# Relational graph layer on one core: nine masks instead of ten, and the mean taken off by ScalarE for a third of the dense tiles and for the finished rows

## The reference

```python
proj = einsum('ni,rio->nro', x, relation_weight)          # 10 matrices of 64 x 64
t_r, h_r = proj[src, etype], proj[dst, etype]
att = sum(t_r * tanh(h_r + edge_attr), -1)
a = softmax of att over the edges of one dst
h = segment_sum(x[src] * a, dst)                          # 0 for a node without edges
y = x + leaky((x + h) @ W.T) + leaky((x * h) @ W2.T)      # slope 0.01
out = (y - mean(y)) / sqrt(var(y) + 1e-5)                 # over the 64 values of a row
```

## Time and profile before

| | |
|---|---|
| median of 3 runs | 757.59 us (756.48 to 757.81) |
| the profiled execution | 757.37 us, its span 755.7 us |
| busy: PE, PEld, DVE, ACT, POOL | 567.3, 310.8, 628.0, 484.1, 569.9 us |
| mean granted TensorE clock | 0.930 |

### The profile page before, as it was taken

How to read it: one execution, slowest core, us unless ns; L and a number is a source line. 1 busy time by engine, 2 the same in 40 slices (tenths; PEclk the granted TensorE clock), 3 DMA queues, 4 the chain that set the end, 5 groups by cost and what they waited for, 6 DMA issues and landing times. The chain is left out here.

```text
span 755.7 us, 14910 instructions
## 1 busy us (share of the span) xinstructions
PE 567.3 (75%) x3948; PEld 310.8 (41%) x3948; DVE 628.0 (83%) x1118; ACT 484.1 (64%) x1432; POOL 569.9 (75%) x590
## 2 busy tenths in 40 slices
PE   1897888888888898888898796899988898853000
PEld 0652454454454454454454453444444443542000
DVE  2689899999999999999999999999998898862010
ACT  0376777778778788779779778655543555665040
POOL 6777777777777777777777777767777777777776
PEclk9999999999999999999999999999999999975555
DMA  4463434444434434434434424320222212100000
GB/s 120 112 188 83 122 99 138 113 110 137 124 100 138 124 96 139 124 97 141 134 85 147 113 56 123 98 77 28 76 76 74 75 37 80 45 27 18 18 18 16
DMA packets 49458, 70.44 MB, mean 93 GB/s; under 512 B 17450, under 2 KB 20966, under 8 KB 49374
## 3 DMA queue, kind: packets, MB, share of 16 engines
q1 hardware_dynamic: 30750, 52.33, 21.5%
q0 software_dynamic: 18624, 17.16, 11.0%
HBM read 45.61 MB, written 25.78 MB: 94 GB/s over the span
## 5 line engine op out<-in xcount | busy, mean ns | idle before, releaser
L454 POOL DMA_INDIRECT xsd<-in_x,ends_i x384 | 374.5, 975 | 118.0 <-issue 109.1
L556 PE MATMUL t_ps<-xm,w_rel 64*64 64x512 f32 (+1 forms) x1000 | 269.5, 621 | 42.0 <-DVE xm L963 41.2
L963 DVE SCALAR_TENSOR_TENSOR xm<-typ,xT_ps 128x1024 f32<-128x1024 f32 (+1 forms) x250 | 291.6, 1183 | 7.2 <-issue 7.2
L558 PE MATMUL h_ps<-xm,w_rel 64*64 64x512 f32 (+1 forms) x1000 | 269.5, 621 | 0.0
L478 POOL DMA_INDIRECT out<-out_r,row_i x196 | 192.3, 981 | 62.5 <-issue 56.7
L556 PEld LDWEIGHTS t_ps<-xm,w_rel 64*64 64x64 f32 x1000 | 52.8, 134 | 144.7 <-DVE xm L963 120.4
L573 PE MATMUL y_ps<-bd_cat,dT 128*128 128x256 f32 x392 | 97.0, 391 | 17.6 <-DVE zd L1025 14.9
L731 ACT ACTIVATE o_t<-zd,rstd 128x64 f32<-128x64 f32 x392 | 98.8, 337 | 15.4 <-DVE rstd L1047 15.3
L573 PEld LDWEIGHTS y_ps<-bd_cat,dT 128*128 128x128 f32 x392 | 71.8, 193 | 30.8 <-issue 12.9
L1005 DVE SCALAR_TENSOR_TENSOR es<-es,wd,wx 128x64 f32<-128x64 f32 x196 | 55.2, 281 | 11.2 <-DVE es L1005 0.5
L738 ACT ACTIVATE wd<-delta 128x16 f32<-128x16 f32 (+1 forms) x25 | 5.4, 216 | 88.2 <-DVE delta L993 83.8
(11 more groups left out here) (155 smaller groups left out, 844.8 us busy)
## 6 DMA issues: line engine op xcount, KB each, us to landing
xsd<-in_x SPq DMA_DIRECT2D x1024, 0.2 KB
x_in<-in_x SPq DMA_DIRECT2D x48, 256.0 KB
typ<-typ_d SPq DMA_DIRECT2D x24, 512.0 KB, 4.8
out<-o_t SPq DMA_DIRECT2D x48, 256.0 KB
xsd<-in_x,ends_i POOLq DMA_INDIRECT x384
hist<-es SPq DMA_DIRECT2D x24, 256.0 KB, 2.0
ea<-in_edge_attr SPq DMA_DIRECT2D x24, 224.0 KB
out<-out_r,row_i POOLq DMA_INDIRECT x196, 2.1
```

Of the source, the lines that this page charges most:

```text
L454: pool.indirect_dma_start(xsd[:, s % RX, j, side, :], None, x[:, :], bass.IndirectOffsetOnAxis(ap=ends_i[:, side, c:c + 1], axis=0),).then ...
L556: pe.matmul(t_ps[h * D:(h + 1) * D, 0:n], w_rel[0:D, r, :], xm[0:D, b, h * n:(h + 1) * n], start=(r == 0), stop=(r == R - 1), skip_group_c ...
L558: mm = pe.matmul(h_ps[(1 - h) * D:(2 - h) * D, 0:n], w_rel[D:P, r, :], xm[D:P, b, (1 - h) * n:(2 - h) * n], start=False, stop=(r == R - 1) ...
L963: v.scalar_tensor_tensor(xm[:, (s * R + r) % RM, 0:n], typ[:, s % RT, 0:n], float(r), xT_ps[:, 0:n], ALU.is_equal, ALU.mult).then_inc(mask ...
```

## The change

1. **Nine masks.** Since the ten types cover every edge, the sum over the ten masked products is x times `w_rel[9]` for all columns, plus the masked products of types 0 to 8 with `w_rel[r] - w_rel[9]`. The differences are made once at the start by DVE (`dif_done`, 128 x 576 elements). In each step ACT copies the whole of `xT_ps` (1024 columns) to a new tile `xc` (`plain(s)`, right after `tanh`), mask 0 waits for that copy instead of for `xT_done`, and PE's fifth quad of the step multiplies `xc`. PE's work keeps its size.
2. **Squares with a bias.** For the third tile of each step (`UNCENTRED`) and for the finished rows no mean is subtracted by DVE. ACT squares `zsum - 64 z`, 8 instructions of 64 columns with the row sum as bias, in place of one of 512; the other squares get the scale 64, and the root 1/64**3.
3. **The mean in the scaling.** A new small DVE instruction `shifts(s)` (128 x 32) gives -mean x rstd; `rec_done` now comes from it, one mask after the reciprocal. `dense_norm` of third tiles and `final_out` use `Identity` with scale and bias in place of `Copy` with scale.
4. `zf` becomes a ring of 3, and the sums stay in `zsum`, with waits for their readers.

```diff
+RF = 3
...
+    RB = R - 1
+    PLAIN_AT = 4
+
+    def quad_count(m):
+        return m // RB * R + m % RB + (2 if m % RB >= PLAIN_AT else 1)
+
+    UNCENTRED = [2]
+
+    def mids(d):
+        return sum(n % 3 not in UNCENTRED for n in range(d + 1))
...
+        xc = sb("xc", [P, COLS * P])
...
-                wait(pe, masked, s * R)
+                wait(pe, masked, s * RB)
...
-            def quad(s, r):
-                pe.wait_ge(masked, s * R + r + 1)
-                if r == 0:
+            def quad(s, at):
+                plain = at == PLAIN_AT
+                r = RB if plain else at - (at > PLAIN_AT)
+                if plain:
+                    pe.wait_ge(plain_done, s + 1)
+                else:
+                    pe.wait_ge(masked, s * RB + r + 1)
+                if at == 0:
                     wait(pe, prod_done, s)
-                b = (s * R + r) % RM
                 n = cols(s) // 2 * P
+                moving = xc[:, :] if plain else xm[:, (s * RB + r) % RM, :]
+                w = w_rel[:, r, :]
                 for h in range(2):
-                    pe.matmul(t_ps[h * D:(h + 1) * D, 0:n], w_rel[0:D, r, :], xm[0:D, b, h * n:(h + 1) * n],
-                              start=(r == 0), stop=(r == R - 1), skip_group_check=True)
-                    mm = pe.matmul(h_ps[(1 - h) * D:(2 - h) * D, 0:n], w_rel[D:P, r, :], xm[D:P, b, (1 - h) * n:(2 - h) * n],
-                                   start=False, stop=(r == R - 1), skip_group_check=True)
+                    pe.matmul(t_ps[h * D:(h + 1) * D, 0:n], w[0:D, :], moving[0:D, h * n:(h + 1) * n],
+                              start=(at == 0), stop=(at == R - 1), skip_group_check=True)
+                    mm = pe.matmul(h_ps[(1 - h) * D:(2 - h) * D, 0:n], w[D:P, :], moving[D:P, (1 - h) * n:(2 - h) * n],
+                                   start=False, stop=(at == R - 1), skip_group_check=True)
                 mm.then_inc(quad_done, 1)
...
+            pe.wait_ge(dif_done, 1)
...
+            def plain(s):
+                n = cols(s) * P
+                act.wait_ge(xT_done, s + 1)
+                wait(act, quad_done, (s - 1) * R + PLAIN_AT + 1 if s > 0 else 0)
+                act.copy(xc[:, 0:n], xT_ps[:, 0:n]).then_inc(plain_done, 1)
...
-                act.wait_ge(zmid_done, d + 1)
                 wait(act, dred_done, d - 1)
-                act.activation(sqd[:, d % 2, :], zd[:, d % RZ, :], ACT.Square).then_inc(dsq_done, 1)
+                if d % 3 in UNCENTRED:
+                    act.wait_ge(zsum_done, d + 1)
+                    for j in range(DR):
+                        ins = act.activation(sqd[:, d % 2, j * D:(j + 1) * D], zd[:, d % RZ, j * D:(j + 1) * D], ACT.Square,
+                                             scale=-float(D), bias=zsum[:, d // 3 % 2, d % 3, j:j + 1])
+                    ins.then_inc(dsq_done, 1)
+                else:
+                    act.wait_ge(zmid_done, mids(d))
+                    act.activation(sqd[:, d % 2, :], zd[:, d % RZ, :], ACT.Square, scale=float(D)).then_inc(dsq_done, 1)
 
             def dense_norm(d):
                 s = d // 3
                 act.wait_ge(rec_done, s + 1)
                 wait(act, o_stored[d % RO], d // RO * DMA)
-                for j in range(DR):
-                    ins = act.activation(o_t[:, d % RO, j * D:(j + 1) * D], zd[:, d % RZ, j * D:(j + 1) * D], ACT.Copy,
-                                         scale=rstd[:, s % 2, d % 3, j:j + 1])
+                if d % 3 in UNCENTRED:
+                    for j in range(DR):
+                        ins = act.activation(o_t[:, d % RO, j * D:(j + 1) * D], zd[:, d % RZ, j * D:(j + 1) * D], ACT.Identity,
+                                             scale=rstd[:, s % 2, d % 3, j:j + 1], bias=shift[:, s % 2, d % 3, j:j + 1])
+                else:
+                    for j in range(DR):
+                        ins = act.activation(o_t[:, d % RO, j * D:(j + 1) * D], zd[:, d % RZ, j * D:(j + 1) * D], ACT.Copy,
+                                             scale=rstd[:, s % 2, d % 3, j:j + 1])
                 ins.then_inc(dmul_done, 1)
...
-                act.activation(sd[:, s % 2, :, :], ssq[:, s % 2, :, :], ACT.Sqrt, scale=1.0 / D, bias=eps_t[:, 0:1]).then_inc(sqrt_done, 1)
+                act.activation(sd[:, s % 2, :, :], ssq[:, s % 2, :, :], ACT.Sqrt, scale=1.0 / D ** 3, bias=eps_t[:, 0:1]).then_inc(sqrt_done, 1)
...
             def final_square(f):
-                act.wait_ge(fsub_done, f + 1)
+                act.wait_ge(fsum_done, f + 1)
                 wait(act, red2_done, f)
-                act.activation(sqf[:, 0:cols(f), :], zcf[:, f % 2, 0:cols(f), :], ACT.Square).then_inc(fsq_done, 1)
+                for j in range(cols(f)):
+                    ins = act.activation(sqf[:, j, :], zf[:, f % RF, j, :], ACT.Square, scale=-float(D),
+                                         bias=zsum[:, f % 2, 3, j:j + 1])
+                ins.then_inc(fsq_done, 1)
 
             def final_out(f, s):
                 act.wait_ge(rec_done, s + 1)
                 if f >= RW:
                     act.wait_ge(scattered[f % RW], sum(cols(n) for n in range(f % RW, f, RW)) * DMA)
                 for j in range(cols(f)):
-                    ins = act.activation(out_r[:, f % RW, j, :], zcf[:, f % 2, j, :], ACT.Copy, scale=rstd[:, s % 2, 3, j:j + 1])
+                    ins = act.activation(out_r[:, f % RW, j, :], zf[:, f % RF, j, :], ACT.Identity,
+                                         scale=rstd[:, s % 2, 3, j:j + 1], bias=shift[:, s % 2, 3, j:j + 1])
                 ins.then_inc(fmul_done, 1)
...
+                if 0 <= s < NS:
+                    plain(s)
...
+            v.wait_ge(w_in, 5 * DMA)
+            v.tensor_tensor(w_rel[:, 0:RB, :], w_rel[:, 0:RB, :], w_rel[:, RB:R, :].to_broadcast([P, RB, D]), ALU.subtract).then_inc(dif_done, 1)
...
-                    v.wait_ge(xT_done, s + 1)
+                    v.wait_ge(plain_done, s + 1)
                     v.wait_ge(typ_in[s % RT], turn(s, RT) * DMA)
-                wait(v, quad_done, s * R + r + 1 - RM)
-                v.scalar_tensor_tensor(xm[:, (s * R + r) % RM, 0:n], typ[:, s % RT, 0:n], float(r), xT_ps[:, 0:n],
+                m = s * RB + r
+                wait(v, quad_done, quad_count(m - RM) if m >= RM else 0)
+                v.scalar_tensor_tensor(xm[:, m % RM, 0:n], typ[:, s % RT, 0:n], float(r), xT_ps[:, 0:n],
                                        ALU.is_equal, ALU.mult).then_inc(masked, 1)
...
             def dense_total(d):
                 v.wait_ge(zadd_done, d + 1)
-                v.tensor_reduce(zsd[:, :], zd[:, d % RZ, :].rearrange("p (j f) -> p j f", f=D), AX.X, ALU.add).then_inc(zsum_done, 1)
+                wait(v, rec_done, d // 3 - 1)
+                wait(v, dsq_done, d - 5)
+                v.tensor_reduce(zsum[:, d // 3 % 2, d % 3, :], zd[:, d % RZ, :].rearrange("p (j f) -> p j f", f=D), AX.X,
+                                ALU.add).then_inc(zsum_done, 1)
 
             def dense_centre(d):
                 v.wait_ge(zsum_done, d + 1)
                 z = zd[:, d % RZ, :].rearrange("p (j f) -> p j f", f=D)
-                v.scalar_tensor_tensor(z, zsd[:, :].unsqueeze(2).to_broadcast([P, DR, D]), -1.0 / D, z, ALU.mult, ALU.add).then_inc(zmid_done, 1)
+                v.scalar_tensor_tensor(z, zsum[:, d // 3 % 2, d % 3, :].unsqueeze(2).to_broadcast([P, DR, D]), -1.0 / D, z,
+                                       ALU.mult, ALU.add).then_inc(zmid_done, 1)
...
+                v.reciprocal(rstd[:, s % 2, :, :], sd[:, s % 2, :, :]).then_inc(rstd_done, 1)
+
+            def shifts(s):
+                v.wait_ge(rstd_done, s + 1)
+                v.scalar_tensor_tensor(shift[:, s % 2, :, :], zsum[:, s % 2, :, :], -1.0 / D, rstd[:, s % 2, :, :],
+                                       ALU.mult, ALU.mult).then_inc(rec_done, 1)
...
             def final_sum(f):
                 n = cols(f)
                 v.wait_ge(z2_done, f + 1)
-                v.tensor_reduce(zs[:, 0:n], zf[:, 0:n, :], AX.X, ALU.add).then_inc(fsum_done, 1)
-
-            def final_centre(f):
-                n = cols(f)
-                v.wait_ge(fsum_done, f + 1)
-                wait(v, fmul_done, f - 1)
-                v.scalar_tensor_tensor(zcf[:, f % 2, 0:n, :], zs[:, 0:n].unsqueeze(2).to_broadcast([P, n, D]), -1.0 / D,
-                                       zf[:, 0:n, :], ALU.mult, ALU.add).then_inc(fsub_done, 1)
...
                     restarts(e)
                 if ending:
                     pair(f)
-                if DP is not None:
-                    dense_centre(DP)
                 if main:
                     mask(s, 4)
-                if main:
-                    mask(s, 5)
                 if DP is not None:
                     dense_sum(DP)
                 if D0 is not None:
...
                     sum_one(e, 0)
                     sum_one(e, 1)
                 if main:
-                    mask(s, 6)
```

(46 more changed lines are left out.)

7 lines of the change are left out of this document (2 added, 5 removed).

## The result

The changed kernel takes 787.94 us, median of 4 runs (786.78 to 788.84), beside 757.7 for the kernel before on the same chip (756.48 to 758.19): a ratio of 1.0397, 95% interval 1.0385 to 1.0409. It is 30 us slower. The profiled execution took 787.24 us, its span is 785.5.

What follows compares the result with a forecast made beforehand. POOL's queue was taken to run to the end, with the steps acting only through the store it awaits. 22.8 + 1.6 + 2.4 = 26.8 us took the profiled 757.37 to 784.2, forecast 784, range 770 to 798.

Steps and rivals of the forecast that it cites:

- What bounds: POOL's gathers and scatters run to the end; steps count only through the store POOL awaits, set by tile 46's scaling.
- First stall: In each step DVE waits before `dense_sum(DP)` for ACT's eight-part square of the third tile: 1.04 us.
- second stall: In each step DVE waits before `dense_add(D1)` for ACT's relu, delayed by the finished rows' squares: 2.9 us.
- The small square: On ACT, each 64-column square with a bias costs 0.24 us start to start, about 2.0 us for eight.
- that rival: Small ACTIVATEs with a bias cost 0.30 us, not 0.24: 12 to 13 us more in all, 797; chance 0.12.
- DVE's own work in a step: DVE's queue without stalls falls from 28.28 to 26.1 us: 2.34 goes out, 0.20 for `shifts` comes in.
- Twelve steps: Steps 3 to 14 have all parts of the loss, each 1.9 us longer: 22.8 us in all.
- Step 15's part: Step 15 up to the end of tile 46's scaling grows from 22.2 to 23.8 us: 1.6 more.
- Start and steps 0 to 2: Weight differences at the start, up to 0.8 us, steps 1 and 2 each 1.0 longer, step 0 even: 2.4 together.
- POOL's hole: POOL's wait for the `o_t` store between gathers and scatters, 3.07 us before, grows to some 30 us.
- PACE's marks: PE's pace marks hold back POOL's gathers but add nothing, being reached well before the store lands.
- The other side's floor: If DVE's saving wins, POOL's hole closes and the time is 754.6 us, no better however short the step; chance 0.07.

Runs made afterwards that it cites:

- Experiment 3: The changed kernel with each set of eight small squares replaced by one instruction of 512 columns without a bias: 757.33 us, ratio 0.9995.
- experiment 7: The changed kernel with `Copy` and a scale alone in place of `Identity` with scale and bias: 781.49 us, ratio 1.0226.
- experiments 1: The kernel before with only the first part of the change (nine masks, plain copy, weight differences): 757.36 us, ratio 0.999.
- 4: The kernel before with nine masks and no mean taken off any dense tile (`dense_centre` gone): 760.61 us, ratio 1.0035.
- 12: The kernel before with only the first part of the change, and `final_out` moved ahead of `weights` in ACT's queue: 757.45 us, ratio 0.999.

## Why the prediction was right

The forecast of 784 stands beside 787.9 measured, and by its own steps:

- **What bounds.** Right: the end moved with the store of tile 48, through the end of tile 46's scaling (501.40, from 499.38 + 2.02 on ACT; predicted near 497) and SP's 24.3 us (24.4). From the first scatter to the end 256.5 in place of 257.8: 196 scatters took 191.0 us, 1.3 less than in the earlier trace rows.
- **First stall** 1.04 predicted, 0.95 measured; **second stall** 2.9 predicted, 3.28 measured. Both stand before the instructions named. Experiment 3 shows that the squares cause the first, and 1.7 us of the second (1.55 stay without them).
- **The small square** 0.24 from start to start: 2.00 to 2.01 for eight, with the bias from a tile. Right; for the squares that rival is out. It named `Identity` with both operands as well, and there it was half right: 2.74 for eight. The Trainium skill, page "ScalarE: Activation LUTs", section "Rules for kernel authors", would have 0.35 us each as an estimate. The trace has a mean duration of 0.33 to 0.34 for one, and 0.24 from start to start, since neighbours overlap: the estimate is near for the duration, and I was wrong to take it as the price of one in a row when I put the page's forecast 20 us later.
- **`shifts`** 0.20 predicted, 0.18. DVE's own work in a step 26.1 predicted, and 26.1 measured (30.34 less the two stalls). **`plain`** cost nothing, as said; it takes 1.01 us.
- **Twelve steps**: 22.8 predicted, 27.8 measured. This is the term that was too small. 2.9 of the 5.0 are four steps with parts at the lower granted clock (31.16, 30.94, 31.21 and 30.97 beside 30.34 for an undisturbed one). 0.8 is on the side of before, whose twelve steps averaged 28.21 and not the 28.28 that I had taken from the earlier trace rows, a stretch that begins in step 8, the one long step (28.56). The rest, 1.3, has two parts of opposite sign. `Identity` with two operands from tiles was costed like `Copy` with a scale; without it the step is 0.30 us shorter (30.04 beside 30.34, experiment 7), 3.0 us over ten steps. And that 30.04 is 0.16 under the 30.2 of my sum, some 1.9 over twelve steps. That they nearly cancel, and put 30.2 beside 30.34, was luck.
- **Step 15's part** 1.6 predicted, 1.5 (23.70 beside 22.19). **Start and steps 0 to 2** 2.4 predicted, 2.1.
- **POOL's hole.** Wrong: 9.11 us, not some 30. I had named PACE's marks as no term of the sum, and that holds. But the delay is spread: the gathers' busy time grew by 6.6 us and the idle time before them by 18.4, together 25.0, which is what the last gather came later (518.94 beside 493.89). The hole shows only what is left.
- **The other side's floor.** Wrong by 3 us: 754.6 supposed that POOL's last gather stays at 493.89 when steps get shorter. In experiments 1, 3, 4 and 12 it came at 497.4 to 500.3, mostly since single gathers took longer (983 to 988 ns on average, beside 975), and their medians are 757.3 to 760.6. So the hole of 2.77 us was not there to be gained, and a shorter step gives nothing.

Open: what lengthens single gathers, what brings on the lower clock in some steps of some kernels, and whether `final_out` ahead of `weights` would win back a part of the loss.

## What to carry to other kernels

Moving work from a full engine to one that is 64% busy is decided where the moved work stands in the receiver's queue, not by its share: look for the instruction behind it that the first engine waits for, and for its slack (here 0.12 us). A mean folded into an ACTIVATE's bias turns one instruction of 512 columns into eight, 1.4 us longer, to save 0.6 us on the other engine. And before shortening the steps of one engine, ask whether they set the end at all: where another engine's instructions follow each other after a fixed gap from first to last, as POOL's do here after 0.30 us, that engine is the bound, and shorter steps elsewhere pay nothing.
